# Mixture of experts by gathered tiles: rows with their probabilities, three gather buffers, scatters in pairs, another dispatch order

## The reference, cut to what matters

```python
def moe_ff(x, gate_w, w1, w2, w3):
    xf = x.reshape(b * t, d)                       # 2048 tokens of 256
    scores = xf @ gate_w                           # 8 experts
    topk_scores, topk_idx = jax.lax.top_k(scores, TOPK)      # 2 choices
    topk_probs = jax.nn.softmax(topk_scores, axis=-1)
    weight = jnp.sum(jax.nn.one_hot(topk_idx, EXPERTS, dtype=xf.dtype) * topk_probs[..., None], axis=1)
    h = jax.nn.silu(jnp.einsum('td,edh->eth', xf, w1)) * jnp.einsum('td,edh->eth', xf, w2)
    out_e = jnp.einsum('eth,ehd->etd', h, w3)      # hidden 512
    out = jnp.einsum('etd,te->td', out_e, weight)
```

## Time and profile before

| | us |
|---|---|
| three timed runs | 2594.98 (median), 2593.19, 2597.88 |
| the profiled execution | 2592.92 |
| its span | 2591.2 |
| the mixture, from its first DMA to the end of the span | 2144 to 2591 |
| the loop over tiles, from the first transposes (L2127) | 2217.7 to 2591 |
| busy over the span | PE 80%, DVE 61%, PE weight loads 55%, ACT 33%, POOL 19% |
| busy in 2354 to 2452 us (98 us of the loop) | PE 69.4, DVE 40.8, ACT 41.5, POOL 52.4, at a granted clock of 0.83 |

### The profile page before, as it was taken

The page is one execution under the profiler, slowest core; times in us unless marked ns, Lnnn a source line. Parts: engine busy times, 40 slices in busy tenths (PEclk is TensorE's granted clock), DMA queues, the critical chain, the costliest instruction groups (busy, mean ns, idle before and its releaser), DMA issues. The chain is left out here.

```text
span 2591.2 us, 32139 instructions
## 1 busy us (share of the span) xinstructions
PE 2075.5 (80%) x11320; PEld 1427.1 (55%) x11320; DVE 1575.3 (61%) x3413; ACT 854.9 (33%) x1587; POOL 482.9 (19%) x340
## 2 busy tenths in 40 slices
PE   7899998699999797567655656578999997767765
PEld 4566663588888573344322333234666645767764
DVE  4677761444443336799999999846777715334432
ACT  2355552122222123311131011123555533434442
POOL 0011110633330030011001111000101100455554
PEclk8799999799999998788877878796999998888887
DMA  4111100311100001000000000011111101645552
GB/s 148 44 33 45 44 23 1 130 49 49 47 18 0 17 33 72 9 9 9 8 1 17 8 8 0 0 44 40 39 45 35 35 1 62 193 125 138 133 130 43
DMA packets 52480, 122.07 MB, mean 47 GB/s; under 512 B 14256, under 2 KB 25264, under 8 KB 49520
## 3 DMA queue, kind: packets, MB, share of 16 engines
q1 hardware_dynamic: 42736, 107.37, 13.6%
q0 software_dynamic: 8832, 12.06, 2.9%
q10 hardware_dynamic: 768, 0.79, 0.1%
HBM read 84.00 MB, written 10.49 MB: 36 GB/s over the span
## 5 line engine op out<-in xcount | busy, mean ns | idle before, releaser
L672 DVE CUSTOM_DVE_ANT_0 a_junk<-pair,a_mask 128x512 f32<-128x512 f32 (+3 forms) x768 | 394.3, 551 | 187.6 <-PE pair L519 184.1
L633 ACT ACTIVATE a_prob<-pair 128x512 f32<-128x512 f32 (+3 forms) x768 | 328.9, 496 | 306.3 <-PE pair L543 303.1
L543 PE MATMUL pair<-a_qx,a_kx 98*128 98x512 f32 (+3 forms) x768 | 265.7, 393 | 6.5 <-ACT a_prob L633 6.4
L519 PE MATMUL pair<-a_kx,a_qx 96*128 96x512 f32 (+3 forms) x768 | 246.7, 392 | 22.2 <-DMA a_qx<-a_comp 17.9
L741 PE MATMUL pair<-m_x_hi,m_w_lo 128*128 128x512 f32 x448 | 178.4, 398 | 48.8 <-POOL m_w_lo L805 46.8
L475 POOL TENSOR_SCALAR_AFFINE_SELECT a_prob<-a_prob 128x512 f32<-128x512 f32 x128 | 81.2, 635 | 699.6 <-ACT a_prob L633 699.6
L924 DVE TENSOR_TENSOR m_h<-pair,m_g 128x512 f32<-128x512 f32 x96 | 66.4, 691 | 225.0 <-PE pair L743 224.3
L1265 PE MATMUL pair<-h_stream,r_w_kz 128*128 128x512 f32 x192 | 103.5, 692 | 118.9 <-DVE r_region L1671 113.4
L519 PEld LDWEIGHTS pair<-a_kx,a_qx 96*128 96x128 f32 x768 | 150.8, 204 | 70.0 <-DVE a_mx_raw L672 28.2
L543 PEld LDWEIGHTS pair<-a_qx,a_kx 98*128 98x128 f32 x768 | 143.2, 193 | 74.1 <-ACT a_prob L633 38.7
L742 PE MATMUL pair<-m_x_hi,m_w_hi 128*128 128x512 f32 x448 | 177.1, 395 | 0.0
(11 more groups left out here) (299 smaller groups left out, 4378.6 us busy)
## 6 DMA issues: line engine op xcount, KB each, us to landing
mx_raw<-in_L_ffn_experts SPq DMA_DIRECT2D x69, 512.0 KB
m_raw<-in_L_cond_experts SPq DMA_DIRECT2D x18, 1024.0 KB, 4.8
a_kx<-a_comp SPq DMA_DIRECT2D x96, 128.0 KB, 2.4
a_qx<-a_comp SPq DMA_DIRECT2D x360, 32.0 KB, 2.0
r_w_ring<-in_r_q_w SPq DMA_DIRECT2D x8, 512.0 KB, 3.9
m_raw<-in_L_cond_experts SPq DMA_DIRECT2D x6, 512.0 KB, 3.2
x_stream<-in_x SPq DMA_DIRECT2D x1, 2048.0 KB, 10.8
pr_gates<-in_L_cond_weight SPq DMA_DIRECT2D x1, 2048.0 KB, 14.6
```

Source lines behind the costliest of these rows:

```text
L519: nc.tensor.matmul(first_bank[t % FR][:, 0:c1 - c0], qx[0:PRODUCT, m % 2, a, i * P:(i + 1) * P], kx[0:PRODUCT, m % 3, a // 2, c0:c1], star ...
L543: nc.tensor.matmul(score_bank[t % SR][:, q0:TT], kx[0:ROWS, n % 3, a // 2, j * P:(j + 1) * P], qx[0:ROWS, n % 2, a, h * TT + q0:(h + 1) * ...
L633: nc.scalar.activation(prob[:, i % RING, a, q0:TT], score_bank[t % SR][:, q0:TT], ACT.Exp, scale=SCALE).then_inc(s["b_exp"], 1)
L672: nc.vector.tensor_tensor_reduce(out=junk[:, t % 2, 0:cols], in0=first_bank[t % FR][:, 0:cols], in1=mask[:, m0:m0 + cols], scale=1.0, scal ...
```

## The change

- **Rows carry their probabilities.** A row of `token_rows` is now 260 floats: the 256 of the token, its two expert numbers and its two probabilities, which DVE writes beside the token's copy (two small copies in the dispatch). `value`, its products on POOL and DVE, and the factor of all lanes are gone. In the loop DVE compares the expert numbers of the gathered rows with the tile's expert, multiplies by the probabilities and adds (`shares`, two small instructions in each tile); ACT's scaling waits for that.
- **`place` carries the token number**: 32 DVE instructions of 128x128 (equal, times token) in place of four of 128x1024, in fp32r buffers that belong to the weights of tile 1; the 32 matmuls have 46 columns, both operands in fp32r, and each waits for its own block only.
- **Order of the dispatch.** PE counts the marks after two of the eight transpose groups, no longer after all; ACT computes the exponential after two of the eight copies; SP writes `token_rows` in two DMAs instead of four, issues the weights of tile 1 without waiting for the 32 matmuls, and then the residual as its parts come.
- **Gathers.** There are three `x_in` buffers. POOL issues the gathers of tiles 0, 1 and 2 ahead of the loop.
- **Scatters.** A scatter waits for the pair of the tile before (`sent` at 32 j), not for the half before it.
- **Weight part 2** is split on DVE like the others, between the second product and its low part; POOL keeps no arithmetic in the loop.

The diff, cut:

```diff
+DEPTH = 3
+ROW = D + 2 * CHOICES
...
-        share = c.sb("mx_share", [P, LANES], ctx=ctx)
+        chosen = c.sb("mx_chosen", [P, 2, 2, CHOICES], ctx=ctx)
+        share = c.sb("mx_share", [P, 2, 2], ctx=ctx)
...
+        sq = h_rows[:, :, :].rearrange("p t d -> p (t d)")[:, 0:NT * KD * TT].rearrange("p (t k n) -> p t k n", t=NT, k=KD)
+        later = [w[:, 1, :, :].rearrange("p a n -> p (a n)") for w in (w_hi, w_lo)]
+        places = [later[0].rearrange("p (b l) -> p b l", l=P), later[1][:, 0:PART].rearrange("p (b l) -> p b l", l=P)]
+        hit = later[1][:, PART:PART + BLOCKS * LANES].rearrange("p (b c) -> p b c", c=LANES)
+
+        def place(b):
+            return places[b // 24][:, b % 24, :]
...
+                sp.wait_ge(s["beside"], 2)
+                tokens_out(0)
+                sp.wait_ge(s["expert"], 1)
+                weights_in(0)
+                tokens_out(1)
+                weights_in(1)
+                for q in range(4):
+                    sp.wait_ge(s["x_ev"], 2 * q + 2)
+                    sp.dma_start(x_out[:, 4 * q:4 * q + 4, :], x_rows[:, 4 * q:4 * q + 4, :]).then_inc(s["out_in"], 16)
+                sp.dma_start(spare_out, x_rows[:, 0:2, :]).then_inc(s["out_in"], 16)
+                for j in range(2, NTILE):
+                    weights_in(j)
...
+                turn_out(0, 2)
                 pe.wait_ge(s["hot"], 1)
                 pe.wait_ge(s["score"], NT)
                 nc.tensor.matmul(c.quad[2][:, 0:E * BLOCKS], c.mean_ones[:, :], flat(hot), start=True, stop=True)\
                     .then_inc(s["ranked"], 1)
                 nc.tensor.matmul(c.quad[3][:, 0:E * BLOCKS], rank, flat(hot), start=True, stop=True).then_inc(s["ranked"], 1)
+                turn_out(2, TL // 2)
...
-                pe.wait_ge(s["value_t"], 1)
-                pe.wait_ge(s["value_p"], 1)
+                pe.wait_ge(s["hit"], 1)
                 for b in range(BLOCKS):
...
-                        pe.wait_ge(s["place"], b // 8 + 1)
-                    last = nc.tensor.matmul(c.bank[1][:, 0:2 * LANES], place[:, b, :],
-                                            value[:, b, :, :].rearrange("p v c -> p (v c)"),
+                    pe.wait_ge(s["place"], b + 1)
+                    last = nc.tensor.matmul(c.bank[1][:, 0:LANES], place(b), hit[:, b, :],
...
-                            pe.wait_ge(s["token"], 4)
-                        pe.wait_ge(s["w_lo_down"], j + 1)
+                            pe.wait_ge(s["token"], 3)
+                        pe.wait_ge(s["w_lo"], 3 * j + 3)
...
+                def turn_out(q0, q1):
+                    for q in range(q0, q1):
+                        act.wait_ge(s["h_mm"], q + 1)
+                        nc.scalar.activation(h_rows[:, 2 * q:2 * q + 2, 0:D],
+                                             c.bank[2 + q % 2].rearrange("p (t d) -> p t d", d=D), ACT.Copy).then_inc(s["h_ev"], 1)
+
+                turn_out(0, 2)
                 act.wait_ge(s["gap"], 1)
                 nc.scalar.activation(odds[:, 1, :], odds[:, 0, :], ACT.Exp).then_inc(s["exp"], 1)
+                turn_out(2, TL // 2)
...
+                    if j == 1:
+                        act.wait_ge(s["found"], 1)
...
-                    act.wait_ge(s["token"], 2)
+                    act.wait_ge(s["share"], j + 1)
...
-                pool.wait_ge(s["hit"], 1)
-                nc.gpsimd.tensor_tensor(value[:, :, 0, :], hit, token.unsqueeze(2).broadcast_to([P, BLOCKS, LANES]), ALU.mult)\
-                    .then_inc(s["value_t"], 1)
-
-                def gather(j):
-                    if j >= 2:
-                        pool.wait_ge(s["turned"], j - 1)
+                def gather(j, half):
+                    n = 2 * j + half
+                    if j >= DEPTH:
+                        pool.wait_ge(s["turned"], j - DEPTH + 1)
+                        pool.wait_ge(s["share"], j - DEPTH + 1)
+                    nc.gpsimd.indirect_dma_start(x_in[:, j % DEPTH, half, :], None, rows,
+                                                 bass.IndirectOffsetOnAxis(row_in[:, n:n + 1], 0)).then_inc(got[j % DEPTH], 16)
+
+                def scatter(j, half):
+                    n = 2 * j + half
+                    pool.wait_ge(s["y"], n + 1)
+                    if j:
+                        pool.wait_ge(s["sent"], 32 * j)
+                    nc.gpsimd.indirect_dma_start(out, bass.IndirectOffsetOnAxis(row_out[:, n:n + 1], 0),
+                                                 y[:, j % 2, half * D:(half + 1) * D], None, compute_op=ALU.add)\
+                        .then_inc(s["sent"], 16)
+
+                pool.wait_ge(s["rows_in"], 2 * 16)
+                pool.wait_ge(s["token"], 1)
...
+                        gather(j, half)
+                pool.wait_ge(s["out_in"], 5 * 16)
+                pool.wait_ge(s["token"], 3)
+                for j in range(NTILE):
                     for half in range(2):
-                        n = 2 * j + half
-                        pool.wait_ge(s["y"], n + 1)
-                        if n:
-                            pool.wait_ge(s["sent"], 16 * n)
-                        nc.gpsimd.indirect_dma_start(out, bass.IndirectOffsetOnAxis(row_out[:, n:n + 1], 0),
-                                                     y[:, j % 2, half * D:(half + 1) * D], None, compute_op=ALU.add)\
-                            .then_inc(s["sent"], 16)
-
-                def weight(j):
-                    pool.wait_ge(s["w_hi"], 3 * j + 3)
-                    nc.gpsimd.tensor_tensor(w_lo[:, j % 2, 2, :], raw[:, j % 2, 2 * PART:3 * PART],
-                                            w_hi[:, j % 2, 2, :].bitcast(F32), ALU.subtract).then_inc(s["w_lo_down"], 1)
...
-                for j in range(NTILE):
-                    if j + 2 < NTILE:
-                        gather(j + 2)
-                    if j + 1 < NTILE:
-                        weight(j + 1)
-                    scatter(j)
+                        scatter(j, half)
+                    for half in range(2):
+                        if j + DEPTH < NTILE:
+                            gather(j + DEPTH, half)
...
                 nc.vector.tensor_tensor(prob[:, 1, :], odds[:, 1, :], prob[:, 0, :], ALU.mult).then_inc(s["prob"], 1)
+                dve.wait_ge(s["mm2"], 1)
+                nc.vector.tensor_copy(h_rows[:, :, D:D + CHOICES].rearrange("p t i -> p i t"), idx_f[:, :, :])\
+                    .then_inc(s["beside"], 1)
+                dve.wait_ge(s["prob"], 3)
+                nc.vector.tensor_copy(h_rows[:, :, D + CHOICES:ROW].rearrange("p t i -> p i t"), prob[:, :, :])\
+                    .then_inc(s["beside"], 1)
...
-                dve.wait_ge(s["h_mm"], TL // 2)
                 dve.wait_ge(s["slot"], 1)
-                for q in range(4):
-                    if q == 1:
-                        dve.wait_ge(s["hit"], 1)
-                        dve.wait_ge(s["prob"], 3)
-                        nc.vector.tensor_tensor(value[:, :, 1, :], hit, prob[:, :, :].rearrange("p i t -> p (i t)").unsqueeze(2)
-                                                .broadcast_to([P, BLOCKS, LANES]), ALU.mult).then_inc(s["value_p"], 1)
-                    b = slice(8 * q, 8 * q + 8)
-                    nc.vector.tensor_tensor(place[:, b, :], lane.unsqueeze(1).broadcast_to([P, 8, P]),
-                                            slot[:, 2, b].unsqueeze(2).broadcast_to([P, 8, P]), ALU.is_equal)\
+                for b in range(BLOCKS):
+                    nc.vector.tensor_scalar(place(b), lane, slot[:, 2, b:b + 1], token[:, b:b + 1], ALU.is_equal, ALU.mult)\
                         .then_inc(s["place"], 1)
...
+
+                def shares(j):
+                    dve.wait_ge(got[j % DEPTH], 32 * (j // DEPTH + 1))
+                    if j >= 2:
+                        dve.wait_ge(s["y"], 2 * (j - 1))
+                    nc.vector.scalar_tensor_tensor(out=chosen[:, j % 2, :, :], in0=x_in[:, j % DEPTH, :, D:D + CHOICES],
+                                                   scalar=expert_f[:, j:j + 1], in1=x_in[:, j % DEPTH, :, D + CHOICES:ROW],
+                                                   op0=ALU.is_equal, op1=ALU.mult).then_inc(s["chosen"], 1)
+                    dve.wait_ge(s["chosen"], j + 1)
+                    nc.vector.tensor_reduce(share[:, j % 2, :], chosen[:, j % 2, :, :], AX, ALU.add).then_inc(s["share"], 1)
...
@@ -2448,11 +2465,14 @@
                         tokens(j + 1)
                         weight(j + 1, 1)
                     prod(2 * j + 1)
+                    if j + 1 < NTILE:
+                        weight(j + 1, 2)
                     rest(2 * j + 1)
+                    shares(j)
...
-    rows = nc.dram_tensor("token_rows", [N, D], F32, kind="Internal").ap()
+    rows = nc.dram_tensor("token_rows", [N, ROW], F32, kind="Internal").ap()
```

(17 more changed lines are left out.)

65 lines of the change are left out of this document (20 added, 45 removed).

## The result

| | before | after |
|---|---|---|
| median of the timed runs, us | 2594.09 (4 runs, 2593.06 to 2597.88) | 2551.72 (4 runs, 2549.17 to 2556.25) |
| ratio | | 0.984, 95% interval 0.9822 to 0.9857 |
| span of the profiled execution, us | 2591.2 | 2550.1 |
| first transposes | 2217.66 | 2211.03 |
| transposes of tile 3 | 2245.70 | 2237.86 |

The change makes the kernel 1.6% faster: 42 us, where some 94 were forecast, outside the range. Four pieces carry the difference of the spans: to the first transposes 6.6 us (forecast 16.7), from there to tile 3 1.2 (3.6), the loop 307.93 - 282.84 = 25.1 (64.8), the end 37.6 - 29.4 = 8.2 (8). They add to 41.1 us. The loop is where most of it went wrong.

What follows compares the result with a forecast made beforehand. The loop was taken as bound by a latency, PE waiting for gathers behind scatters, not by an engine. Loop 64.8, dispatch 16.7, to tile 3 3.6 and end 8 sum to 93.1 us off 2592.92: 2500 us, range 2458 to 2545.

Steps and rivals of the forecast that it cites:

- Gathers three ahead: Mixture loop: a third gather buffer leaves the gathers behind the scatters, so it was given 0 us.
- the circle: Loop's chain of waits: transposes, down projection, result, scatter, gather, next transposes; one makes one tile, 16.21 us before.
- The rival of the broken circle: Loop: gathers no longer wait behind results, PE is the bound at 9.4 us a tile; 2434 us, chance 0.04.
- The turn: Loop: time from one tile's transposes to the next's, forecast to fall from 16.21 to 12.8 us.
- The pair, 2.75 us less: Loop: the second scatter starts 1.9 us after the first instead of 4.64, 2.75 us less in each tile.
- Weight part 2 from POOL to DVE: Loop: a third 1.22 us split on DVE, not a bound; waits of gather issues for DVE taken as 0.4 us a turn.
- the mean landing g: Loop: second gather from its start until landed, mean 3.53 us, between 2.73 and 4.75.
- PE's part: Loop: from a tile's transposes to the start of the next result, taken as 3.01 us, 2.13 at full clock.
- The dispatch, 16.7 us: Ahead of the loop: first transposes at 2201 instead of 2217.66, 16.7 us less, bounds 8 and 20.
- To tile 3, 3.6 us: From the first transposes to those of tile 3: 24.4 us instead of 28.04, 3.6 us less.
- The end, 8 us: From the transposes of tile 22 to the end: 28.6 to 30.6 us instead of 37.6, 8 us less.
- The collisions rival: Loop: POOL's issues collide with DVE in every tile and the clock falls; turn 14.4 us, 2536 us, chance 0.18.

Runs made afterwards that it cites:

- the loads-held run: The changed kernel, with SP holding the loads of weight parts 1 and 2 until the gather under way has landed: 2502.94 us, ratio 0.9638 to the kernel before.
- the run with part 2 on POOL: The changed kernel with the split of weight part 2 put back on POOL, behind the gathers: 2514.91 us, ratio 0.97 to the kernel before.

## Why the prediction was wrong

*Gathers three ahead bring nothing by themselves: right.* The six gathers stand ahead of the first scatter pair, PE still waits for each gather, and the circle closes as before. The third buffer was not tried by itself. The rival of the broken circle named 2434 us and 9.4 us a tile; one swap of two loops gives 2434.34 and 9.50. The turn was understood; that the time meets to the microsecond is luck, since the profiled execution took 2441.07 and the dispatch in it saved 9.3 us, not 17.

*The pair, 2.75 us less: right.* The starts lie 1.93 us apart (forecast 1.9), no wait for a landing is left, and alone it makes the turn 12.88 us.

*Weight part 2 from POOL to DVE, and with it the mean landing g: this step failed.* I asked what the added split costs DVE (nothing, right: DVE is busy 47.8 of 100 us) and what it costs POOL's issues (0.4 us), and took the landing's mean over from the kernel before. I did not ask what the split releases. It releases a buffer, so the load of 512 KB moves from behind the gathers to beside them. Busy us, granted clock, DMA share and GB/s of 2350 to 2450 us, the kernel after:
```profile
2350.00:2450.00 100.00, 73.91 (x507) 72.46 (x506) 47.82 (x69) 43.21 (x66) 37.84 (x27) 0.84 0.56 148
```
A DMA share of 0.56 looks harmless, as a mean: it is the overlap in the 5 us behind the gathers that counts. The landing grew to 5.20 us. The forecast had 3.53 + 0.04 + 0.4 = 3.97; that is 1.23 of the 2.09 us by which the turn is longer than forecast. Another 0.50 is PE's part, 3.51 us instead of 3.01: PE stands 3.8 us in each tile in the mean, and in 14 of 20 tiles its transposes run in 1.07 to 1.12 us, at the lower of its two clock levels, where in the loads-held run 16 of 20 take 0.65 or 0.66. The last 0.36 us lies between the result and the second gather: from the first gather's start to the second's it is 1.55 us in the mean, where the sum had 1.31, and three gaps are 0.03 to 0.05 us longer. The sum had taken 1.01 us for the first gather's issue from one row; the mean is 1.24 (1.20 before). Over 19 turns it is 39.7 us of the 52 by which the forecast for the profiled execution was off; 10.1 lie ahead of the first transposes and 2.4 from there to tile 3.

The Trainium skill has the rule that I should have weighed (DMA: Bandwidth & Descriptors, "Queues, rings and completion order"): each DMA engine goes round the queue rows it has work for, a packet from each in turn. The traces agree: both queues have packets in the same stretch, and the landing is 5.20 us with two loads starting beside it, 3.60 with none, whether they are left out or held. The rule of the Trainium skill that I did weigh (SBUF — State Buffer, "SBUF: two separate sides") has the descriptors locked out while DVE runs an instruction in its 2-port mode, and speaks of issues. These didn't grow as forecast: the mean issue of a gather is 1.26 us before and 1.27 after.

My reading of the earlier trace rows was off as well: the issue of 1.99 us waited for the split that was under way at its start, till 2325.48, and not for `h_lo` behind it. From tile 3 on the twelve traces agree on this: where no split and no `h_lo` of DVE runs as the issue starts, it takes 0.95 to 1.04 us, also when one starts just behind; where one is under way with more than 0.15 us to go, it ends 0.82 to 0.90 us after that one (243 of 245 issues).

*The dispatch, 16.7 us: right in kind, 15.0 in size, of which the profiles show 6.6.* The timeline of the kernel after, the marks, the exponential, the scan, the placing and the matmuls:
```profile
2182.99 0.43 DVE L2349 TENSOR_TENSOR mx_hot<-mx_const,mx_idx_f 128x256 f32<-128x256 f32 x1
...
2185.29 0.22 ACT L2216 ACTIVATE mx_odds<-mx_odds 128x16 f32<-128x16 f32 x1
...
2186.34 0.68 DVE L2367 TENSOR_TENSOR_SCAN mx_before<-mx_const,pair 128x256 f32<-128x256 f32 x1
...
2192.82 6.24 DVE L2412 TENSOR_SCALAR mx_w_hi<-mx_const,mx_slot 128x128 fp32r<-128x128 f32 x24
...
2196.33 3.07 PE L2127 MATMUL pair<-mx_w_lo,mx_w_hi 128*128 128x46 f32 x24
2199.37 2.20 PE L2127 MATMUL pair<-mx_w_lo 128*128 128x46 f32 x8
```
From the start of the marks to the first transposes it is 28.0 us, against 43.1 before. Scan after marks: 3.35 us instead of 7.63. The 32 matmuls: 5.2 us instead of 13.9; the instructions that feed them take 0.26 us each, not the 0.19 of my estimate, inside its bounds. But the marks themselves came 8.4 us later than in the earlier trace rows, of which 5.3 us lie ahead of all that is changed, and the scoring matmuls ran 11.5 instead of 8.5 us. That is a scatter between executions and not the change: the scoring matmuls take 8.4 to 8.5 us in two of the four profiled kernels with the old dispatch and 11.5 in the other two, and with the new one 8.5 us in two and 11.1 to 11.5 in the other six. From the marks to the first transposes the four old ones take 43.1 to 43.6 us and the eight new ones 27.9 to 28.5, so the dispatch is worth 15.2 us. The four old ones reach the first transposes at 2217.7 to 2224.9, mean 2222.6, the eight new ones at 2204.0 to 2213.0, mean 2208.9.

*To tile 3, 3.6 us:* it was 1.2 (26.83 us instead of 24.4). The landing of this tile, 3.51 us, was as forecast. The first result came 0.6 us later, and from there to the second gather it took 7.7 us, not 5.8: the first scatter started 0.6 us later after the result, the second's issue took 2.33 us and the first gather's 1.47. *The end, 8 us:* it was 8.2. The last two scatters of the kernel after start 1.86 us apart, 10 us before the end:
```profile
2540.44 1.56 POOL L2301 DMA_INDIRECT out_rows<-mx_y,mx_row_out  x1 [3.36 <-ACT mx_y L2262]
2542.30 1.56 POOL L2301 DMA_INDIRECT out_rows<-mx_y,mx_row_out  x1 [0.30 <-issue]
```
*The rivals.* The collisions rival came nearest in size (14.4 us a turn, 2536 us), but by another mechanism: I had bounded what could hold up the gathers by POOL's issues and by the clock, not by the DMA engines. The greatest landing of my own rows, 4.75 us, was used as an end of g and not in the range of its mean. The rate of 0.12 us after the stand of 1.87 us isn't in the two starts of the earlier trace rows, which are 0.22 apart; the matmuls that follow them in the trace do start 0.12 us apart.

## What to carry to other kernels

A split, a copy or a cast that is moved to another engine also moves the moment at which its source buffer is free, and so the next transfer into it: list what each moved instruction releases, and see which latency on the circle that transfer falls beside. In a loop whose bound is a latency, look first at whether an order keeps the request behind the result: swapping two loops gave 117 us over the changed kernel, moving the split between engines gave or cost 37 to 38. An edit's sign can turn when the bound changes, so each is measured again after the bound is gone.

## What the runs showed of the hardware

A gather of 128 rows, which lands in 3.60 us from the start of its issue, takes 5.20 in the mean when two loads of 512 KB start beside it; holding the loads until it has landed cost nothing, since PE waited for no weight in that run. A scatter that adds took 7.8 us from its start to the next beside three such loads, instead of 4.64; that the loads are the cause is read from one trace and was not tried by itself. The issue of a gather on POOL waits for the end of a DVE subtraction of two SBUF inputs that is under way (1.99 us instead of 1.01 in the earlier trace rows), and not for one that starts later. DVE's split of 1.22 us took 2.70 when POOL ran its own split beside it, in the run with part 2 on POOL:
```profile
2350.78 2.70 DVE L2435 TENSOR_TENSOR mx_w_lo<-mx_raw,mx_w_hi 128x1024 fp32r<-128x1024 f32 x1
```
The idle stretch of PE alone doesn't tell the clock level of the transposes behind it: in the kernel after, 14 tiles ran them in 1.07 to 1.12 us after stands of 3.1 to 5.1 us, and 6 tiles in 0.66 us after stands of 3.0 to 3.7.
